# Local attention stage: softmax division moved from VectorE to GpSimd, norm floor by a second reduction, loop body of one group instead of two

## The chip, the cores and the metric

The kernel runs on one core of one Trainium2 chip. The metric is the device time of one execution, in microseconds (us); the number reported is the median of several runs. In what follows PE is TensorE (PEld its weight loads), DVE is VectorE, ACT is ScalarE, POOL is GpSimd and SP is SyncE, whose queue issues DMAs.

## The reference

The program keeps a residual x of 128 sequences of 64 tokens with 128 features and runs four pairs of layers over it: cross attention with a low-rank expert layer, with a mixture of experts, with a channel mixer, and last with two layers of local attention and a gated MLP. Only the local attention is touched by the change. It runs twice (DEPTH = 2), with 8 heads of 64 features:

```python
def l2norm(t):
    return t / jnp.clip(jnp.linalg.norm(t, axis=-1, keepdims=True), 1e-12)

def _layer(x, wqkv, qs, ksc, wo, lg, lb, w1, b1, w2, b2):
    h = shift_token(x)              # second half of the features from the token before
    q, k, v = jnp.split(h @ wqkv, 3, axis=-1)       # each b, 8 heads, n, 64
    q = l2norm(q) * qs
    k = l2norm(k) * ksc
    q, k = rotary_xpos(q, k)        # q * table_a + rotate_half(q) * table_b, the same for k
    o = local_attention(q, k, v)    # window 64 = the sequence: causal, softmax(8 * q k^T) @ v
    x = x + o @ wo
    ...                             # then the gated MLP, which the change leaves alone
```

## The kernel before

x stays in SBUF as 64 tiles of 128 rows (two sequences of 64 tokens) by 128 features. A group is 4 tiles (GT = 4), so there are 16 groups. `local_attention(l)` (from L1726) is written once per engine: each engine has a `body(g, par)` that loops over u = 0 to 3, and each step u works on several tiles at once, as a software pipeline over tiles. Tile n is the one whose attention ends in this step; n+1, n+2 and n+3 are in earlier phases. Engines meet only through semaphores (`wait_tile`), each engine does its work strictly in the order in which it is written, and that order is the only thing that sets the order of the work.

The way of one tile, with the names and lines as they stand in the profile:

- SP copies a group of x, with the shifted halves, into `hi` (the tensor `ci`), two buffers in turn (`move_shifted`, L1603, L1605). PE transposes the group into `bank_p` (L1788) and ACT copies it to `q_t` (L1902), two buffers in turn.
- `project_qk` (PE, L1796, L1797) writes q and k, 128x1024 in PSUM. `squares` (ACT, L1907) squares them. DVE multiplies them by the rotary tables: `rotate` (L2011) and two `cross` (L2018); POOL adds both (`unite`, L1970).
- `sum_squares` (DVE) sums the squares of each head (L2023) and then takes the maximum with 1e-24 and multiplies by 2^20 in one small instruction on 128x16 (L2026). `roots` (ACT, L1912, L1915) turns that into an inverse root by Ln and Exp, `refine_root` (POOL, L1976 to L1980) refines it in four small steps, and `scale_qk` (POOL, L1988) multiplies the rotated q and k with it. This last one gives the semaphore `unit`.
- `turn_qk` (PE, L1817) transposes q and k, `copy_qk` (ACT, L1926) copies them to SBUF, `scores` (PE, L1828 and L1836) multiplies them and adds the causal mask.
- The softmax: `maxima` (DVE, L2034), `shift` (DVE, L2039), `exponentials` (ACT, L1930), and `sums` (DVE), which is the sum (L2047), its reciprocal (L2049) and the division, a multiplication of 128x512 by the reciprocals (L2051).
- `turn_probs` (PE, L1847), `copy_pt` (ACT, L1935), `project_v` (PE, L1807) with `copy_v` (ACT, L1920), `weigh_values` (PE, L1861), `copy_ot` (ACT, L1940), `project_o` (PE, L1869), and `residual` (DVE, L2056).

Inside the stage, `run_pipeline` (L480 to L495) unrolls the first bodies and the last ones and runs the middle in a hardware loop whose body is two groups, 8 tiles, because the buffers of the groups alternate. The loop runs 7 times.

Of the kernel before, what the change touches and what calls it, by code (L numbers as in the profile page):

```python
# [85 lines left out]
def build_program(nc, w, x_in, ctx_t, mask_l2, mask_l3, out):  # L86

    with ExitStack() as ctx:
# [38 lines left out]
        big_flat = sb("big_flat", [P, 7 * INNER])  # L127
# [68 lines left out]
        top8 = sb("top8", [P, GT, 8])  # L196

# [1399 lines left out]
        def move_shifted(sp, last=False):  # L1597

            half = P // 2

            def load(g, par):
                rows = bass.ds(g * GT, GT)
                sp.dma_start(hi[par][:, :, 0:half], x[:, rows, 0:half]).then_inc(shift_loaded.sem, 16)  # L1603
                for b in range(2):
                    sp.dma_start(hi[par][b * S + 1:(b + 1) * S, :, half:P],  # L1605
                                 x[b * S:(b + 1) * S - 1, rows, half:P]).then_inc(shift_loaded.sem, 16)
# [4 lines left out]
            def body(g, par):  # L1611
# [7 lines left out]
                load(g + 2, par)  # L1619
# [17 lines left out]
        def prepare_layers():  # L1637

            with nc.Block() as block:
# [7 lines left out]
                def _(dve):  # L1647
                    for l in range(DEPTH):
# [77 lines left out]
        def local_attention(l):  # L1726
# [31 lines left out]
            nwork, nrm, nlog, nroot, nstep = (small[n][:, 0, :] for n in "abcde")  # L1758
# [15 lines left out]
            with nc.Block() as block:  # L1774
                @block.sync
                def _(sp):
                    move_shifted(sp)

                @block.tensor
                def _(pe):  # L1780
                    def tokens(t, par):
                        return q_t[(par + t // GT) % 2][:, t % GT * P:(t % GT + 1) * P]

                    def transpose_window(g, par):
                        pe.wait_ge(shift_loaded.sem, shift_loaded.at(g, 48))
                        wait_tile(pe, pt_copied, g, -GT)
                        for u in range(GT):
                            last = pe.transpose(bank_p[:, u * P:(u + 1) * P], hi[par][:, u, :], ident[:, :])  # L1788
                        last.then_inc(xt_in_psum.sem, 1)

                    def project_qk(g, t, par):
# [4 lines left out]
                        pe.matmul(bank_qk[:, 0, :], tokens(t, par), w_qkv[l][:, 0:INNER], start=True, stop=True)  # L1796
                        pe.matmul(bank_qk[:, 1, :], tokens(t, par), w_qkv[l][:, INNER:2 * INNER],  # L1797
                                  start=True, stop=True).then_inc(qk_in_psum.sem, 1)

                    def project_v(g, t, par):  # L1800
                        wait_tile(pe, v_copied, g, t - 1)
                        pe.sem_inc(pe_turn.sem, 1)
                        h = tokens(t, par)
# [46 lines left out]
                    def weigh_values(g, t):  # L1850
# [22 lines left out]
                    def body(g, par):  # L1873
                        for u in range(GT):
                            now, next_ = has_tile(g, u), has_tile(g, u + 1)
                            if has_tile(g, u + 3):
                                project_qk(g, u + 3, par)
                            if next_:
                                scores(g, u + 1)
                            if now:  # L1880
                                turn_probs(g, u)
                            if next_:
                                project_v(g, u + 1, par)
                            if now:
                                weigh_values(g, u)
                            if u == 0 and has(g + 1):
                                transpose_window(g + 1, 1 - par)
# [5 lines left out]
                    run_pipeline(pe, body, 1)  # L1893

                @block.scalar
                def _(act):
                    act.preload_act_table_set(LN_EXP)

                    def copy_window(g, par):
                        act.wait_ge(xt_in_psum.sem, xt_in_psum.at(g, 1))  # L1900
                        wait_tile(act, v_in_psum, g, -GT - 1)
                        act.activation(q_t[par][:, :], bank_p, ACT.Copy).then_inc(xt_ready.sem, 1)  # L1902
# [39 lines left out]
                    def body(g, par):  # L1942
# [398 lines left out]
```

## Time and profile before

| | us |
|---|---|
| median of 3 runs (lowest, highest) | 3454.64 (3454.24, 3457.28) |
| the profiled execution | 3454.24 |
| its span, first to last instruction | 3452.6 |
| PE busy in the span | 3039.5 (88%) |
| DVE busy | 2674.7 (77%) |
| ACT busy | 1624.8 (47%) |
| POOL busy | 895.3 (26%) |
| mean granted clock of TensorE | 0.951 of full speed |

The busy shares are over the whole program, of which the two local attentions are about a third: they stand at 2044 to 2585 us and at 2736 to 3298 us of the span. What holds a stage is read from that stretch alone, and in a pipeline over tiles from the time between equal instructions of neighbouring tiles. A row of the timeline gives an instruction's start and its duration; neighbouring DVE instructions overlap by some 0.1 us, so the cost of one in a full queue is the distance from its start to the start of the next.

### The profile page before, as it was taken

The numbers are of one execution on the slowest core, as the hardware profiler recorded it, in microseconds if no ns is written. First come the engines' busy times: TensorE is split into PE (matmuls) and PEld (weight loads), VectorE is DVE, ScalarE is ACT, GpSimd is POOL, SyncE is SP. The second block draws the span as 40 slices with busy tenths as digits, with TensorE's granted clock in tenths as the row PEclk, the third lists the DMA queues.
The fourth block names the chain that finished last, engine by engine and source line by source line (L and its number), as shares of the span: only waits on it lengthen the run. The fifth ranks groups of instructions, "written<-read, shape, count | busy, mean of one in ns | idle before, by whom it ended". The sixth has DMA issues, their size and how long they took to land. (4 is left out here: it accounts for less than half of the span.)

```text
span 3452.6 us, 95073 instructions
## 1 busy us (share of the span) xinstructions
PE 3039.5 (88%) x34096; PEld 2055.4 (60%) x34128; DVE 2674.7 (77%) x5823; ACT 1624.8 (47%) x2545; POOL 895.3 (26%) x940
## 2 busy tenths in 40 slices
PE   4999668998999979998799938898889888888889
PEld 2666555665666646666566626666655465656655
DVE  5887776886777757776588859999986599899965
ACT  2665214654333335553356625555553355555533
POOL 1000000000000000000100036666652266666634
PEclk9999668998999989999899969999999999999999
DMA  4111001110000011110011110000001100000022
GB/s 141 30 29 22 0 3 29 29 29 10 1 0 0 0 29 41 40 38 2 16 27 29 28 58 11 8 7 9 6 4 32 23 11 8 11 8 11 2 70 76
DMA packets 193348, 80.30 MB, mean 23 GB/s; under 512 B 179155, under 2 KB 182149, under 8 KB 192517
## 3 DMA queue, kind: packets, MB, share of 16 engines
q1 hardware_dynamic: 191876, 73.38, 9.1%
q0 software_dynamic: 1280, 4.20, 0.3%
q8 instruction: 142, 2.33, 0.3%
q14 instruction: 50, 0.40, 0.0%
HBM read 35.71 MB, written 8.39 MB: 13 GB/s over the span
## 5 line engine op out<-in xcount | busy, mean ns | idle before, releaser
L768 ACT ACTIVATE probs_t<-ps_pt 128x1024 f32<-128x1024 f32 x256 | 262.2, 1024 | 385.5 <-PE ps_pt L882 385.5
L630 DVE TENSOR_REDUCE row_max<-ps_s 128x16 f32<-128x1024 f32 x256 | 313.1, 1223 | 135.4 <-PE ps_s L871 132.4
L1970 POOL TENSOR_TENSOR kblk<-kblk 128x1024 f32<-128x1024 f32 x128 | 301.5, 2356 | 191.1 <-DVE kblk L2011 191.1
L635 DVE TENSOR_TENSOR probs<-ps_s,row_max 128x1024 f32<-128x1024 f32 x256 | 311.9, 1218 | 11.7
L614 POOL TENSOR_TENSOR x<-x,out_bias_L 128x512 f32 (+1 forms) x32 | 40.7, 1271 | 1028.4 <-DVE x_norm L424 519.8
L904 PE MATMUL ps_o<-v,probs_t 128*64 128x18 f32 x8192 | 285.1, 212 | 5.4 <-issue 5.2
L904 PEld LDWEIGHTS ps_o<-v,probs_t 128*64 128x64 f32 x8192 | 259.7, 138 | 40.3 <-issue 18.8
L882 PE MATMUL ps_pt<-ident,probs 128*128 128x128 f32 x2048 | 277.1, 278 | 3.1 <-ACT probs L763 3.1
L871 PE MATMUL ps_s<-kblk,q_t 64*64 64x512 f32 x2048 | 271.7, 603 | 7.0 <-issue 7.0
L763 ACT ACTIVATE probs<-probs 128x1024 f32<-128x1024 f32 x256 | 269.7, 1053 | 15.6 <-DVE probs L635 14.1
L1988 POOL TENSOR_TENSOR kblk<-kblk,small_d 128x1024 f32<-128x1024 f32 x128 | 243.6, 1903 | 50.6 <-POOL small_d L1980 50.6
L882 PEld LDWEIGHTS ps_pt<-ident,probs 128*128 128x128 f32 x2048 | 223.1, 141 | 36.7 <-issue 23.8
L1560 POOL TENSOR_TENSOR probs<-probs 128x512 f32<-128x512 f32 x16 | 16.8, 1048 | 866.6 <-ACT probs L1537 866.6
L2018 DVE TENSOR_TENSOR kblk<-ps_s,rot 128x512 f32<-128x512 f32 x256 | 173.5, 679 | 31.7 <-ACT probs L1907 31.6
L1325 ACT ACTIVATE probs<-ps_s 128x512 f32<-128x512 f32 x128 | 76.5, 597 | 226.3 <-PE ps_pt L1272 170.7
L2026 DVE TENSOR_SCALAR small_b<-small_a 128x16 f32<-128x16 f32 x128 | 169.7, 1326 | 15.0
L1817 PE MATMUL ps_s<-ident,kblk 128*128 128x128 f32 x1024 | 139.3, 280 | 38.2 <-POOL kblk L1988 37.1
L1926 ACT ACTIVATE big_flat<-ps_s 128x1024 f32<-128x1024 f32 x128 | 131.3, 1026 | 82.0 <-PE ps_s L1817 82.0
L1907 ACT ACTIVATE probs<-ps_s 128x1024 f32<-128x1024 f32 x128 | 131.0, 1024 | 79.4 <-PE ps_s L1797 75.1
L1869 PE MATMUL ps_pj<-w_lo,big_flat 128*128 128x128 f32 x1024 | 138.8, 279 | 32.1 <-ACT big_flat L1940 32.1
L1281 PEld LDWEIGHTS ps_o<-w,probs 128*128 128x128 f32 x1024 | 133.0, 191 | 49.5 <-issue 25.5
L891 PEld LDWEIGHTS ps_pt<-ident,o 128*128 128x128 f32 x256 | 35.4, 138 | 212.1 <-issue 123.3
(305 smaller groups left out, 6879.2 us busy)
## 6 DMA issues: line engine op xcount, KB each, us to landing
ci<-in_ctx_t SPq DMA_DIRECT2D x64, 256.0 KB, 3.0
kblk<-k_t SPq DMA_DIRECT2D x768, 16.0 KB
ci<-x SPq DMA_DIRECT2D x64, 128.0 KB
ci<-x SPq DMA_DIRECT2D x128, 63.0 KB
x<-in_x_in SPq DMA_DIRECT2D x4, 1024.0 KB, 8.1
mask<-in_mask_l SPq DMA_DIRECT2D x64, 64.0 KB, 2.5
kblk<-ci SPq DMA_DIRECT2D x256, 16.0 KB
out<-x SPq DMA_DIRECT2D x1, 4096.0 KB, 11.1
```

What stands on the lines that cost most here:

```text
L630: dve.tensor_reduce(row_max[u % 2][:, :], scores_of(u), AX, ALU.max).then_inc(max_ready.sem, 1)
L635: dve.tensor_tensor(probs[u % 2][:, :, :], scores_of(u), row_max[u % 2][:, :].unsqueeze(2).broadcast_to([P, HEADS, S]), ALU.subtract).then ...
L763: act.activation(p, p, ACT.Exp, scale=scale).then_inc(exp_ready.sem, 1)
L768: act.activation(probs_t[:, :, :], ps_pt[:, :, :].rearrange("p a (r t) -> p (a r) t", t=P), ACT.Copy).then_inc(pt_ready.sem, 1)
L871: last = pe.matmul(bank[b * S:(b + 1) * S, c, :], q_t[par][rows, tok], kblk[par][rows, :, tok], start=plain, stop=True, skip_group_check=n ...
L882: last = pe.transpose(ps_pt[:, r // 4, (r % 4) * P:(r % 4 + 1) * P], flat[:, r * P:(r + 1) * P], ident[:, :])
L904: last = pe.matmul(accumulated[half, 2 * r:2 * r + 2, :], probs_t[:, r, half], v2[par][:, 2 * u + b, r, :, :], start=True, stop=True)
L1817: last = pe.transpose(bank_ts[:, i, r * P:(r + 1) * P], rotated_qk[t % 2][:, i * INNER + r * P:i * INNER + (r + 1) * P], ident[:, :])
L1970: pool.tensor_tensor(a, a, b_, ALU.add).then_inc(rotated.sem, 1)
L1988: pool.tensor_tensor(a, a, nroot.unsqueeze(2).broadcast_to([P, 2 * LHEADS, LD]), ALU.mult)\
L2018: dve.tensor_tensor(b_[:, :, :, to:to + HALF], by_half(bank_qk)[:, :, :, of:of + HALF], table(1, to, HALF), ALU.mult).then_inc(products.se ...
L2026: dve.tensor_scalar(nrm, nwork, 1e-24, float(2 ** LOG_SCALE), ALU.max, ALU.mult)\
```

## The change

Six things change, all in `local_attention` or for it:

1. The division goes from DVE to POOL: `sums` ends with the reciprocal, and a new `scale_probs` (POOL) multiplies the 128x512 probabilities. The reciprocals have two places in turn.
2. The floor of the norms is no longer a `tensor_scalar` (maximum, then times 2^20) but a second `tensor_reduce` with maximum over pairs: the sums are written to column 0 of the new tensor `floored` (128x16x2), whose column 1 holds 1e-24. The factor 2^20 goes into ACT's Ln (as its scale) and into POOL's third refining step.
3. The order of DVE: maxima, shift, sums and reciprocal of tile n+1 in one stretch, then rotate, cross, cross and the norms of tile n+3; before, the two were interleaved.
4. The order of PE and ACT: `turn_probs` of tile n+1 ends a step (before, that of tile n stood behind the scores), scores come first, and V is projected and copied three tiles ahead, beside q and k, where it was one tile ahead. So `v_rows` needs four places instead of two; they are put over `kblk0`, and `big_flat` shrinks from 7 to 5 blocks.
5. POOL's `refine_root` and `scale_qk` become one `normalise_qk` for tile n+2, with two semaphore increments fewer.
6. `run_tiles` replaces `run_pipeline` here: a loop of one group (4 tiles) that runs 14 times, with one buffer `hi[0]` and one `q_t[0]` instead of two; SP's `move_window` loads a group once the one before it is transposed.

```diff
-            nwork, nrm, nlog, nroot, nstep = (small[n][:, 0, :] for n in "abcde")
+            nrm, nlog, nroot, nstep = (small[n][:, 0, :] for n in "bcde")
...
+        def run_tiles(eng, body):
+            for g in range(-1, 1):
+                body(g)
+            with eng.Fori(1, GROUPS - 1) as g:
+                body(g)
+            body(GROUPS - 1)
...
+        def move_window(sp):
+            def body(g):
+                if has(g + 1):
+                    if has(g):
+                        sp.wait_ge(xt_in_psum.sem, xt_in_psum.at(g, 1))
+                        sp.sem_inc(sp_turn.sem, 1)
+                    load_shifted(sp, g + 1, 0)
...
                 def _(dve):
+                    dve.memset(floored[:, :, 1], 1e-24).then_inc(tables.sem, 1)
...
-                                    at = t % 2 * INNER + b * 2 * P + r * LD
+                                    at = t % GT * INNER + b * 2 * P + r * LD
...
                     def roots(g, t):
                         wait_tile(act, norms, g, t)
-                        act.activation(nlog, nrm, ACT.Ln).then_inc(l_root.sem, 1)
+                        act.activation(nlog, nrm, ACT.Ln, scale=float(2 ** LOG_SCALE)).then_inc(l_root.sem, 1)
...
                     def copy_v(g, t):
                         wait_tile(act, v_in_psum, g, t)
-                        wait_tile(act, summed, g, t - 2)
-                        act.activation(v_rows[:, t % 2 * INNER:(t % 2 + 1) * INNER], bank_v, ACT.Copy)\
+                        wait_tile(act, summed, g, t - GT)
+                        act.activation(v_rows[:, t % GT * INNER:(t % GT + 1) * INNER], bank_v, ACT.Copy)\
...
-                    def body(g, par):
+                    def body(g):
                         for u in range(GT):
-                            now, soon = has_tile(g, u), has_tile(g, u + 2)
-                            if soon:
-                                roots(g, u + 2)
+                            now, next_ = has_tile(g, u), has_tile(g, u + 1)
+                            if next_:
+                                exponentials(g, u + 1)
                             if has_tile(g, u + 3):
                                 squares(g, u + 3)
                             if now:
-                                copy_pt(g, u)
+                                copy_ot(g, u)
+                            if has_tile(g, u + 3):
+                                copy_v(g, u + 3)
                             if u == 0 and has(g + 1):
-                                copy_window(g + 1, 1 - par)
-                            if has_tile(g, u + 1):
-                                exponentials(g, u + 1)
-                            if now:
-                                copy_ot(g, u)
-                            if soon:
+                                copy_window(g + 1)
+                            if has_tile(g, u + 2):
                                 copy_qk(g, u + 2)
-                            if has_tile(g, u + 1):
-                                copy_v(g, u + 1)
+                            if has_tile(g, u + 3):
+                                roots(g, u + 3)
+                            if next_:
+                                copy_pt(g, u + 1)
...
+                    def scale_probs(g, t):
+                        wait_tile(pool, rec_ready, g, t)
+                        pool.sem_inc(pool_turn.sem, 1)
+                        inverse = row_max[1][:, t % 2 * LHEADS:(t % 2 + 1) * LHEADS]
+                        p3 = by_head(pl)
+                        pool.tensor_tensor(p3, p3, inverse.unsqueeze(2).broadcast_to([P, LHEADS, S]), ALU.mult)\
+                            .then_inc(p_scaled.sem, 1)
...
-                        dve.tensor_reduce(nwork, square, AX, ALU.add).then_inc(norms.sem, 1)
+                        dve.tensor_reduce(floored[:, :, 0], square, AX, ALU.add).then_inc(norms.sem, 1)
                         wait_tile(dve, norms, g, t, 1)
                         wait_tile(dve, l_newton, g, t - 1)
-                        dve.tensor_scalar(nrm, nwork, 1e-24, float(2 ** LOG_SCALE), ALU.max, ALU.mult)\
-                           .then_inc(norms.sem, 1)
+                        dve.tensor_reduce(nrm, floored[:, :, :], AX, ALU.max).then_inc(norms.sem, 1)
```

How the instructions of one tile stand on three engines before and now, in the middle of the stage. POOL first: `kblk` holds the rotated q and k, `small_d` and `small_e` the root and its refining step, `big_flat` the probabilities. Before:

```order
L1988 TENSOR_TENSOR kblk<-kblk,small_d 128x1024 [waits l_newton,rotated]
L1970 TENSOR_TENSOR kblk<-kblk 128x1024 [waits products]
L1976 TENSOR_TENSOR small_e<-small_d 128x16 [waits l_root]
L1977 TENSOR_TENSOR small_e<-small_e,small_b 128x16 [waits l_newton]
L1979 TENSOR_SCALAR small_e<-small_e 128x16 [waits l_newton]
L1980 TENSOR_TENSOR small_d<-small_d,small_e 128x16 [waits l_newton]
```

and now, with the probabilities' scaling in front of the addition of tile n+2:

```order
L1993 TENSOR_TENSOR big_flat<-big_flat,row_max 128x512 [waits rec_ready]
L2000 TENSOR_TENSOR kblk<-kblk 128x1024 [waits products]
L2006 TENSOR_TENSOR small_e<-small_d 128x16 [waits l_root]
L2007 TENSOR_TENSOR small_e<-small_e,small_b 128x16 [waits l_newton]
L2009 TENSOR_SCALAR small_e<-small_e 128x16 [waits l_newton]
L2010 TENSOR_TENSOR small_d<-small_d,small_e 128x16 [waits l_newton]
L2013 TENSOR_TENSOR kblk<-kblk,small_d 128x1024 [waits rotated,l_newton]
```

One instruction of 128x512 is added, between two big ones that were neighbours. On DVE, one step before:

```order
L2034 TENSOR_REDUCE row_max<-ps_s 128x8 [waits scored]
L2018 TENSOR_TENSOR kblk<-ps_s,rot 128x16x32 [waits rotated,l_squared]
L2039 TENSOR_TENSOR big_flat<-ps_s,row_max 128x2x4x64 [waits turned,max_ready]
L2018 TENSOR_TENSOR kblk<-ps_s,rot 128x16x32 [waits rotated,l_squared]
L2011 TENSOR_TENSOR kblk<-ps_s,rot 128x1024 [waits qk_turned,l_squared]
L2023 TENSOR_REDUCE small_a<-probs 128x16 [waits l_squared]
L2026 TENSOR_SCALAR small_b<-small_a 128x16 [waits l_newton,norms]
L2047 TENSOR_REDUCE row_max<-big_flat 128x8 [waits exp_ready]
L2049 RECIPROCAL row_max<-row_max 128x8 [waits sums_ready]
L2051 TENSOR_TENSOR big_flat<-big_flat,row_max 128x512 [waits rec_ready]
L2056 TENSOR_TENSOR x<-x,ps_pj 128x128 [waits y_ready]
```

and now:

```order
L2057 TENSOR_REDUCE row_max<-ps_s 128x8 [waits scored]
L2060 TENSOR_TENSOR big_flat<-ps_s,row_max 128x2x4x64 [waits turned,max_ready]
L2068 TENSOR_REDUCE row_max<-big_flat 128x8 [waits p_scaled,exp_ready]
L2070 RECIPROCAL row_max<-row_max 128x8 [waits sums_ready]
L2036 TENSOR_TENSOR kblk<-ps_s,rot 128x1024 [waits qk_turned,l_squared]
L2043 TENSOR_TENSOR kblk<-ps_s,rot 128x16x32 [waits rotated,l_squared] x2
L2048 TENSOR_REDUCE floored<-probs 128x16 [waits l_squared]
L2051 TENSOR_REDUCE small_b<-floored 128x16 [waits l_newton,norms]
L2074 TENSOR_TENSOR x<-x,ps_pj 128x128 [waits y_ready]
```

The division (L2051 of before) is gone, the floor (L2026) is now a reduction (L2051 of the change), and the sum waits for `exp_ready` right behind the shift that ACT's exponential needs. On PE, one step before:

```order
L1796 MATMUL ps_s<-w_qkv,q_t 128x512
L1797 MATMUL ps_s<-w_qkv,q_t 128x512
L1828 MATMUL ps_s<-mask_causal,ident 64x256 x4
L1836 MATMUL ps_s<-big_flat 64x64 x16
L1847 MATMUL ps_pt<-ident,big_flat 128x128 x4
L1807 MATMUL ps_pt<-w_qkv,q_t 64x256 x4
L1861 MATMUL ps_o<-big_flat 64x64 x16
L1817 MATMUL ps_s<-ident,kblk 128x128 x8
L1869 MATMUL ps_pj<-w_lo,big_flat 128x128 x4
```

and now:

```order
L1851 MATMUL ps_s<-mask_causal,ident 64x256 x4
L1859 MATMUL ps_s<-big_flat 64x64 x16
L1819 MATMUL ps_s<-w_qkv,q_t 128x512
L1820 MATMUL ps_s<-w_qkv,q_t 128x512
L1830 MATMUL ps_pt<-w_qkv,q_t 64x256 x4
L1884 MATMUL ps_o<-big_flat,kblk 64x64 x16
L1840 MATMUL ps_s<-ident,kblk 128x128 x8
L1892 MATMUL ps_pj<-w_lo,big_flat 128x128 x4
L1870 MATMUL ps_pt<-ident,big_flat 128x128 x4
```

The same instructions in the same number; the transposition of the probabilities (L1847, now L1870) went from behind the scores to in front of the next tile's scores, and q, k and V of one tile now stand together.

## Rows read from the trace of the kernel before

**Rows 1.** The projections of q in the first and in the second local attention.

```profile
L1796 PE MATMUL ps_s<-w_qkv,q_t x128: 592/595/1222, 2049.9 to 2559.5; 128*128 128x512 f32 x128
...
L1796 PE MATMUL ps_s<-w_qkv,q_t x128: 592/595/1222, 2741.4 to 3271.9; 128*128 128x512 f32 x128
```

**Rows 2.** Timeline of DVE, one tile: start us, duration us, engine, line, operation.

```profile
2301.10 0.67 DVE L2047 TENSOR_REDUCE row_max<-big_flat 128x8 f32<-128x512 f32 x1
...
2302.04 0.69 DVE L2051 TENSOR_TENSOR big_flat<-big_flat,row_max 128x512 f32<-128x512 f32 x1
2302.65 0.28 DVE L2056 TENSOR_TENSOR x<-x,ps_pj 128x128 f32 x1
...
2305.34 1.21 DVE L2011 TENSOR_TENSOR kblk<-ps_s,rot 128x1024 f32<-128x1024 f32 x1
2306.47 1.21 DVE L2023 TENSOR_REDUCE small_a<-probs 128x16 f32<-128x1024 f32 x1
2307.82 1.30 DVE L2026 TENSOR_SCALAR small_b<-small_a 128x16 f32<-128x16 f32 x1
2309.03 0.67 DVE L2047 TENSOR_REDUCE row_max<-big_flat 128x8 f32<-128x512 f32 x1
...
2311.70 0.69 DVE L2034 TENSOR_REDUCE row_max<-ps_s 128x8 f32<-128x512 f32 x1 [0.84 <-PE ps_s L1836]
...
2312.91 0.68 DVE L2039 TENSOR_TENSOR big_flat<-ps_s,row_max 128x512 f32<-128x512 f32 x1
```

**Rows 3.** Timeline of POOL, one tile.

```profile
2306.73 2.35 POOL L1970 TENSOR_TENSOR kblk<-kblk 128x1024 f32<-128x1024 f32 x1 [0.96 <-DVE kblk L2011]
2309.86 0.22 POOL L1976 TENSOR_TENSOR small_e<-small_d 128x16 f32<-128x16 f32 x1 [0.77 <-ACT small_d L1915]
2310.16 0.59 POOL L1977 TENSOR_TENSOR small_e<-small_e,small_b 128x16 f32<-128x16 f32 x1
...
2311.80 1.91 POOL L1988 TENSOR_TENSOR kblk<-kblk,small_d 128x1024 f32<-128x1024 f32 x1 [0.35 <-POOL small_d L1980]
```

**Rows 4.** Timeline of PE, one tile without a group's transposition.

```profile
2309.05 1.02 PE L1796 MATMUL ps_s<-w_qkv,q_t 128*128 128x512 f32 x2
...
2310.86 0.30 PE L1828 MATMUL ps_s<-mask_causal,ident 64*64 64x256 bf16 x4
...
2311.56 0.65 PE L1847 MATMUL ps_pt<-ident,big_flat 128*128 128x128 f32 x4
2312.14 1.08 PE L1807 MATMUL ps_pt<-w_qkv,q_t 128*64 128x256 f32 x8
...
2314.24 1.09 PE L1817 MATMUL ps_s<-ident,kblk 128*128 128x128 f32 x8
2315.17 1.07 PE L1869 MATMUL ps_pj<-w_lo,big_flat 128*128 128x128 f32 x8
2316.07 0.59 PE L1796 MATMUL ps_s<-w_qkv,q_t 128*128 128x512 f32 x1
```

**Rows 5.** Timeline of ACT, two of its instructions there.

```profile
2310.97 1.02 ACT L1907 ACTIVATE probs<-ps_s 128x1024 f32<-128x1024 f32 x1 [1.28 <-PE ps_s L1797]
...
2313.62 0.63 ACT L1930 ACTIVATE big_flat<-big_flat 128x512 f32<-128x512 f32 x1 [0.78 <-DVE big_flat L2039]
```

**Rows 6.** DMA queue of instructions, 2040 to 2590 us and then 2740 to 3300 us.

```profile
q8 instruction: 13, 0.21, 0.2%
...
q8 instruction: 67, 1.10, 0.8%
```

**Rows 7.** Timeline of DVE and POOL side by side, normalising the residual before this stage.

```profile
2021.35 5.32 POOL L1692 TENSOR_TENSOR x<-x,probs 128x3072 f32<-128x3072 f32 x1 [11.60 <-DMA out<-x]
2021.38 10.64 DVE L1714 TENSOR_TENSOR x<-x,probs 128x5120 f32<-128x5120 f32 x1 [9.35 <-DMA out<-x]
```

**Rows 8.** Groups by line: a small DVE reduction, a full-stream POOL addition.

```profile
L1185 DVE TENSOR_REDUCE tiny_f<-small_b 128x4 f32<-128x16 f32 x16 | 2.7, 170 | 0.5
...
L2161 POOL TENSOR_TENSOR x<-x,b_dn 128x512 f32 x24 | 30.3, 1264 | 55.4 <-DVE x_norm L451 49.0 <-DMA ci<-x 6.4
```

More of the change, by code:

```diff
@@ L1595, in build_program, with load_shifted @@
         shift_loaded = signal("shift_loaded")
-        def move_shifted(sp, last=False):
[L1599 to L1606, printed above, removed]
+        def load_shifted(sp, g, par):
+            half = P // 2
+            rows = bass.ds(g * GT, GT)
+            sp.dma_start(hi[par][:, :, 0:half], x[:, rows, 0:half]).then_inc(shift_loaded.sem, 16)
+            for b in range(2):
+                sp.dma_start(hi[par][b * S + 1:(b + 1) * S, :, half:P],
+                             x[b * S:(b + 1) * S - 1, rows, half:P]).then_inc(shift_loaded.sem, 16)
+        def move_window(sp):
[5 more added lines that the diff above has]
+                    load_shifted(sp, g + 1, 0)
+            sp.wait_ge(first_rows.sem, 4)
+            run_tiles(sp, body)
+        def move_shifted(sp, last=False):
             def fetch(g, par):
@@ L1618, in body @@
                 sp.sem_inc(sp_turn.sem, 1)
-                load(g + 2, par)
+                load_shifted(sp, g + 2, par)
                 if last:
@@ L1776, in _, with tokens, transpose_window @@
                 def _(sp):
-                    move_shifted(sp)
+                    move_window(sp)
                 @block.tensor
                 def _(pe):
-                    def tokens(t, par):
-                        return q_t[(par + t // GT) % 2][:, t % GT * P:(t % GT + 1) * P]
-                    def transpose_window(g, par):
+                    def tokens(t):
+                        return q_t[0][:, t % GT * P:(t % GT + 1) * P]
+                    def transpose_window(g):
                         pe.wait_ge(shift_loaded.sem, shift_loaded.at(g, 48))
@@ L1787, in transpose_window, with project_qk @@
                         for u in range(GT):
-                            last = pe.transpose(bank_p[:, u * P:(u + 1) * P], hi[par][:, u, :], ident[:, :])
+                            last = pe.transpose(bank_p[:, u * P:(u + 1) * P], hi[0][:, u, :], ident[:, :])
                         last.then_inc(xt_in_psum.sem, 1)
-                    def project_qk(g, t, par):
+                    def project_qk(g, t):
                         if t % GT == 0:
@@ L1795, in project_qk, with project_v @@
                         wait_tile(pe, squared, g, t - 1)
[L1796 to L1797 removed]
+                        pe.matmul(bank_qk[:, 0, :], tokens(t), w_qkv[l][:, 0:INNER], start=True, stop=True)
+                        pe.matmul(bank_qk[:, 1, :], tokens(t), w_qkv[l][:, INNER:2 * INNER],
                                   start=True, stop=True).then_inc(qk_in_psum.sem, 1)
[L1800 removed]
+                    def project_v(g, t):
                         wait_tile(pe, v_copied, g, t - 1)
                         pe.sem_inc(pe_turn.sem, 1)
[L1803 removed]
+                        h = tokens(t)
                         w_v = w_qkv[l][:, 2 * INNER:3 * INNER].rearrange("p (r j d) -> p r j d", j=2, d=LD)
@@ L1897, in _, with copy_window @@
                     act.preload_act_table_set(LN_EXP)
-                    def copy_window(g, par):
+                    def copy_window(g):
                         act.wait_ge(xt_in_psum.sem, xt_in_psum.at(g, 1))
-                        wait_tile(act, v_in_psum, g, -GT - 1)
-                        act.activation(q_t[par][:, :], bank_p, ACT.Copy).then_inc(xt_ready.sem, 1)
+                        wait_tile(act, v_in_psum, g, -1)
+                        act.activation(q_t[0][:, :], bank_p, ACT.Copy).then_inc(xt_ready.sem, 1)
                     def squares(g, t):
@@ L1978, in refine_root @@
                         pool.sem_inc(pool_turn.sem, 1)
-                        step(pool.tensor_scalar(nstep, nstep, -0.5, 1.5, ALU.mult, ALU.add))
+                        step(pool.tensor_scalar(nstep, nstep, -0.5 * 2 ** LOG_SCALE, 1.5, ALU.mult, ALU.add))
                         step(pool.tensor_tensor(nroot, nroot, nstep, ALU.mult))
-                    def scale_qk(g, t):
                         wait_tile(pool, rotated, g, t)
-                        pool.sem_inc(pool_turn.sem, 1)
-                        wait_tile(pool, l_newton, g, t)
-                        pool.sem_inc(pool_turn.sem, 1)
                         a = by_head(rotated_qk[t % 2])
@@ L2223, in build_program @@
         qk_t = flat_big[:, 0:2 * INNER].rearrange("p (i t) -> p i t", i=2)
-        v_rows = flat_big[:, 2 * INNER:4 * INNER]
-        pl, pt, ot = (flat_big[:, i * INNER:(i + 1) * INNER] for i in (4, 5, 6))
+        pl, pt, ot = (flat_big[:, i * INNER:(i + 1) * INNER] for i in (2, 3, 4))
+        v_rows = kblk[0][:, :, :].rearrange("p h t -> p (h t)")[:, 0:GT * INNER]
         flat_parts = kblk[1][:, :, :].rearrange("p h t -> p (h t)")
```

67 lines of the change are left out of this document (29 added, 38 removed).

## Prediction

> **What bounds the kernel now.** The busy shares of the page do not say it: DVE 77%, PE 88% and POOL 26% are averages over eight stages, and the change touches two of them. I read first the line of one instruction that every tile has once, for the rate of the stage: the projection of q starts at 2049.9 for the first tile and at 2559.5 for the last of the first local attention, 509.6 us for 63 steps, 8.09 us a tile; in the second it is 530.5 us, 8.42 a tile [rows 1]. Together 1040.1 us for 126 steps, 8.25 a tile. Then the timeline engine by engine, for what each engine needs for a tile when nothing stops it, from start to start:
>
> - DVE: from one sum to the next, 2301.10 to 2309.03, 7.93 us without a gap [rows 2]. The next step has a wait of 0.84 us for the scores. So DVE is full, and its own 7.93 is nearly the whole 8.09.
> - PE: 2309.05 to 2316.07, 7.02 us for the same work [rows 4], plus a group's transposition (about 0.5) in one tile of four: 7.14. PE is second.
> - POOL: additions and multiplications of 2.35 and 1.91, a chain of four small steps between them, and waits for DVE and ACT [rows 3]. POOL is third.
>
> The second stage has the same engines and the same tiles, but is 20.9 us longer. What differs is the queue that fetches instructions: 13 packets in the first stage, 67 in the second [rows 6], on a loop of 8 tiles that turns 7 times. I read this as the loop's code being kept once and fetched again at each turn the other time, at 20.9 / 7 = 3.0 us a turn.
>
> **What the change does to each engine.** The division costs DVE 0.61 (2302.04 to 2302.65) [rows 2]; it goes. The floor costs it 1.21 (2307.82 to 2309.03), for 16 elements. That is a wait, not work: it ends at 2309.12 and POOL's addition ends at 2306.73 + 2.35 = 2309.08 [rows 2, 3]. Rows of another place show the same exclusion: DVE's subtraction of 5120 elements takes 10.64 beside a POOL operation of 5.32 that began 0.03 before it, where five times the 1.21 of 1024 elements would be 6.05 [rows 7, 2]. The new floor is a reduction of 32 elements to 16. No row shows one of this shape; a reduction of 16 elements takes 0.17 [rows 8] and I take 0.2. If it waits like the old one it costs 1.2; below 0.17 nothing speaks for it. Whether reductions wait is read off L1970: L2023, a reduction in SBUF, begins at 2306.47 and runs to 2307.68, POOL's addition begins inside it at 2306.73 and takes 2.35 for 1024 elements, where the one of L2161 takes 1.26 for 512 [rows 2, 3, 8]. So neither held the other up. DVE then needs 7.93 - 0.61 - 1.21 + 0.2 = 6.31 of work a tile. The new order adds waits, since the sum now stands right behind the shift: the exponential, 0.63 and 0.03 of handover on either side [rows 5], about 0.7; some 0.1 because the shift follows its maxima at once; and 0.1 for the squares, which ACT does after the exponential (1.02 [rows 5] against 0.94 for sum and reciprocal [rows 2]). DVE: 7.2.
>
> The Trainium skill says in "SBUF — State Buffer", section "SBUF: two separate sides", that the second port pair of VectorE is GpSimd's too and is locked for a whole instruction by a VectorE operation in a two-port mode or with two SBUF inputs; its "Vector Engine (DVE) Microarchitecture Reference", 5.1, gives those modes to copy, cast and tensor_scalar alone. By that the old floor waits and neither the reductions nor the reciprocal do, and the trace agrees for L2026 and L2023; by a lock that every SBUF-only operation took, the sum would be that of the slower rival below.
>
> POOL gains the division. It is the form of L1988, a broadcast multiplication, 1.91 for 1024 elements; L1970 and L2161, 2.35 for 1024 elements and 1.26 for 512, leave 0.17 that an instruction costs at any length [rows 3, 8]; (1.91 - 0.17) / 2 + 0.17 is 1.04. The bounds are 0.95 (half of 1.91) and 1.26, a POOL operation on 512 elements with two full streams [rows 8]. The small steps take 1.94 from 2309.86 to 2311.80; of this L1977 has 0.59 where its like L1976 has 0.22, held by DVE's division beside it, so 0.37 goes, and 0.2 of the 0.35 idle before L1988 goes with the two increments [rows 3]: 1.37. POOL: 2.35 + 1.91 + 1.04 + 1.37 + three handovers of 0.2 (the 0.18 below) = 7.27, the fullest engine. Where a page speaks against the change: "GPSIMD Engine Reference" of the Trainium skill, 4.1, sends elementwise work on a tile to VectorE, GpSimd being about twice slower. The row bears out less, 1.04 against 0.69 on DVE, because the second operand is a broadcast; at twice the DVE's 0.69, an estimate from that page, POOL would need 7.6.
>
> PE's work is the same, 7.14. ACT has two passes over 1024 elements at 1.02 and five over 512 at about 0.63 [rows 5], 5.2 with no more than two small ones besides, and is under the others.
>
> **The chain over engines.** Three engines at 7.1 to 7.3 do not run at 7.27 unless no chain between them is longer. The longest that I find goes round in two tiles. It starts when POOL has normalised q and k of tile k (0). PE starts 0.1 later and, in its new order, turns q and k (0.93), projects the output (0.90) and turns the probabilities (0.58) [rows 4]: 2.51, the scores of k begin. Maxima begin 0.84 after the scores [rows 2, 4]: 3.35; shift 0.72 later, 0.68 long [rows 2]: 4.75; exponential 0.03 + 0.63: 5.41; squares of k+2 on ACT 0.03 + 1.02 [rows 5]: 6.46, a little after sum and reciprocal (0.94, 6.38); rotate starts at 6.55 and takes 1.13 (2305.34 to 2306.47), the two crosses 0.60 and 0.68 [rows 2]: 8.96. POOL takes it up 0.18 later (2305.34 + 1.21 to 2306.73), adds 2.35, refines 0.1 + 1.37, multiplies 1.91 [rows 2, 3]: 14.87, the same point for k+2. So 7.43 a tile. In one tile of four ACT also copies the group's transposition (about 0.6) before the q and k that the scores need, of which some 0.45 is late: 0.11 a tile. Sum 7.54; I take 7.55.
>
> V three tiles ahead, its four places, the single `q_t` and `hi` cost nothing: the next group's load is asked for a whole group (30 us) before it is needed, and V's copy is ready three tiles early; without this cover each of the 32 groups would wait for its load, which no row here times. The memset of the floor is 0.1.
>
> **Code.** The loop is now 4 tiles and turns 14 times. Half the code should be kept in either stage, so the 20.9 us go; they are inside the sum, as both stages get 7.55.
>
> **Sum.** 126 x 7.55 = 951.3 against 1040.1: 88.8 less. Filling and draining hang on single chains and stay, 0.3 either way. From the profiled execution's 3454.24 (span 3452.6 and 1.6 around it; the median of the runs is 3454.64, 0.4 above): 3365.7, so 3366.
>
> **Rivals.**
> - *POOL alone sets the rate.* The two-tile chain has slack that I count twice, and all settle at 7.27. For it: my handovers are rounded up. 126 x 7.27 = 916.0: 3330.
> - *The reciprocal waits for POOL.* It is small, one-source and in SBUF like the old floor. At 6.1 of the chain POOL is in its last multiplication or just before; the rate would settle where the reciprocal slips in before it, 6.14 + 1.91 = 8.05. 126 x 8.05 = 1014.3: 3428. For it: no row shows a reciprocal in SBUF beside a long POOL operation. Against: L2023.
> - *The fetches stay.* The second loop is fetched anew at each of 14 turns at 3.0: 42 more: 3408. Against: 13 packets for a loop twice as long [rows 6].
> - *The floor does not get cheaper.* The reduction waits for POOL as the scalar form did, and the change doesn't do what it says: DVE at 7.2 + 1.1 = 8.3, 1045.8 in all: 3460, no change.
> - *Slower: all of DVE's SBUF-only operations exclude POOL.* POOL is busy 6.1 a tile, and the norms' reduction (1.21), the sum (0.67), the reciprocal and the floor (0.2 each) are 2.3. Before, POOL had the room to let them pass; now, with 1.1 of handovers, the tile takes 9.5: 126 x 9.5 = 1197, 157 more: 3611. It decides from 1.0 us of exclusion a tile (8.25 - 7.27). For it: L2026 and L1714 did wait. Against: L1970 beside L2023 did not grow.
>
> **How the numbers follow.** Forecast (7.4 to 7.75 a tile, 3347 to 3391) 0.64; POOL's rate 0.08; the reciprocal 0.11; fetches 0.08; floor 0.05; exclusion 0.04. This kernel's runs tell 0.2% (7 us) from no change. Faster is the forecast and the first three rivals, 0.91; same the floor, 0.05; slower 0.04. The range leaves out the first rival, the floor and the exclusion: 3338 to 3429. The unknown costs lie in it: a POOL division of 1.26 makes POOL 7.49, 0.95 makes it 7.18.
>
> **What would show it.** Starts of q's projection 7.5 us apart on average in both stages and some 30 us a group; DVE's floor at 0.2 and no longer ending with POOL's addition; POOL's division at 1.0 and L1977's like at 0.22; POOL over 90% occupied with waits for DVE's products before the addition; some ten or twenty instruction packets in either stage; no "issue" wait of 2 us before the projections. It is wrong if the reciprocal's rows exceed 0.3, if the floor's reach 1, or if PE's granted clock falls within the stages.

## The result and the profile after

| | before | changed |
|---|---|---|
| median, us (lowest, highest) | 3455.56 (3454.24, 3457.28), 4 runs | 3342.16 (3339.53, 3343.67), 4 runs |
| span of the profiled execution | 3452.6 | 3340.7 |
| mean granted clock of TensorE | 0.951 | 0.949 |

The ratio is 0.9671 (95% interval 0.9654 to 0.9687). The forecast was 3366 in a range of 3338 to 3429: the sign and the mechanism came, the gain was 24 us larger. The time is 4 us inside the range, and 5 us below the band of 3347 to 3391 that the forecast itself stood for. First the rate of the stage, as in [rows 1]:

```profile
L1819 PE MATMUL ps_s<-w_qkv,q_t x128: 592/697/1220, 2048.3 to 2515.0; 128*128 128x512 f32 x128
...
L1819 PE MATMUL ps_s<-w_qkv,q_t x128: 592/697/1222, 2695.8 to 3159.5; 128*128 128x512 f32 x128
```

466.7 and 463.7 us for 63 steps each, 930.4 together, where before there were 1040.1. That is 109.7 of the span's 111.9 us. The rest of the program kept its times. Per tile it is 7.41 and 7.36, against 8.09 and 8.42, and the second stage is no longer slower than the first. The queue that fetches instructions, 2040 to 2560 us and 2700 to 3200 us ([rows 6]), now looks the same in both stages:

```profile
q8 instruction: 10, 0.16, 0.1%
...
q8 instruction: 10, 0.16, 0.1%
```

The timeline of one tile, in the form of [rows 2 to 5], in the order of start times over all engines:

```profile
2320.17 1.05 POOL L1993 TENSOR_TENSOR big_flat<-big_flat,row_max 128x512 f32<-128x512 f32 x1
...
2320.34 1.09 PE L1840 MATMUL ps_s<-ident,kblk 128*128 128x128 f32 x8 [0.32 <-POOL kblk L2013]
...
2322.69 0.30 PE L1851 MATMUL ps_s<-mask_causal,ident 64*64 64x256 bf16 x4
...
2322.83 0.19 DVE L2051 TENSOR_REDUCE small_b<-floored 128x16 f32<-128x32 f32 x1
...
2323.53 0.69 DVE L2057 TENSOR_REDUCE row_max<-ps_s 128x8 f32<-128x512 f32 x1 [0.26 <-PE ps_s L1859]
...
2324.26 0.69 DVE L2060 TENSOR_TENSOR big_flat<-ps_s,row_max 128x512 f32<-128x512 f32 x1
...
2324.38 0.22 POOL L2007 TENSOR_TENSOR small_e<-small_e,small_b 128x16 f32<-128x16 f32 x1
...
2324.99 0.63 ACT L1952 ACTIVATE big_flat<-big_flat 128x512 f32<-128x512 f32 x1 [0.98 <-DVE big_flat L2060]
...
2325.46 1.90 POOL L2013 TENSOR_TENSOR kblk<-kblk,small_d 128x1024 f32<-128x1024 f32 x1 [0.16 <-POOL small_d L2010]
2325.52 1.00 ACT L1929 ACTIVATE probs<-ps_s 128x1024 f32<-128x1024 f32 x1
2325.65 0.69 DVE L2068 TENSOR_REDUCE row_max<-big_flat 128x8 f32<-128x512 f32 x1 [0.69 <-ACT big_flat L1952]
2326.32 1.15 PE L1884 MATMUL ps_o<-big_flat,kblk 64*64 64x64 f32 x32
2326.37 0.20 DVE L2070 RECIPROCAL row_max<-row_max 128x8 f32<-128x8 f32 x1
2326.56 1.23 DVE L2036 TENSOR_TENSOR kblk<-ps_s,rot 128x1024 f32<-128x1024 f32 x1
...
2327.70 1.28 DVE L2043 TENSOR_TENSOR kblk<-ps_s,rot 128x512 f32<-128x512 f32 x2
...
2329.16 2.37 POOL L2000 TENSOR_TENSOR kblk<-kblk 128x1024 f32<-128x1024 f32 x1 [0.79 <-DVE kblk L2043]
```

Three things are to be seen. The floor (L2051) takes 0.19 where it took 1.30, the division on POOL 1.05, and the step L2007 0.22 where L1977 took 0.59 [rows 2, 3]. The reciprocal (L2070) runs at 2326.37 for 0.20, in the middle of POOL's multiplication L2013 (2325.46 to 2327.36): it does not wait for it. And no engine sets the rate alone: DVE waits 0.69 for the exponential, POOL 0.79 for DVE's products, PE 0.32 for POOL. What sets the rate is the ring, the chain of waits through all four engines that comes back to its start.

### The profile page after: what moved, and what is told of

Its sections match the earlier page's. It is cut to its first block and busy times, and to the rows that moved or that the text cites. A ratio compares the mean times of both kernels' runs of the same rounds, so it can differ in the third digit from the quotient of the medians.

```text
span 3340.7 us, 95362 instructions
## 1 busy us (share of the span) xinstructions
PE 3035.8 (91%) x34128; PEld 2065.1 (62%) x34128; DVE 2487.0 (74%) x5696; ACT 1605.6 (48%) x2545; POOL 968.2 (29%) x1068
## 5 line engine op out<-in xcount | busy, mean ns | idle before, releaser
L2013 POOL TENSOR_TENSOR kblk<-kblk,small_d 128x1024 f32<-128x1024 f32 x128 | 243.5, 1902 | 19.0 <-POOL small_d L2010 17.7
L2036 DVE TENSOR_TENSOR kblk<-ps_s,rot 128x1024 f32<-128x1024 f32 x128 | 156.8, 1225 | 33.5 <-ACT probs L1929 33.5
L2043 DVE TENSOR_TENSOR kblk<-ps_s,rot 128x512 f32<-128x512 f32 x256 | 163.7, 681 | 0.0
L1884 PEld LDWEIGHTS ps_o<-big_flat,kblk 64*64 64x64 f32 x4096 | 129.6, 134 | 51.3 <-issue 51.3
L2068 DVE TENSOR_REDUCE row_max<-big_flat 128x8 f32<-128x512 f32 x128 | 87.8, 686 | 94.0 <-ACT big_flat L1952 94.0
L2048 DVE TENSOR_REDUCE floored<-probs 128x16 f32<-128x1024 f32 x128 | 154.7, 1209 | 0.0
```

Of the source, the lines that this page charges most:

```text
L2013: pool.tensor_tensor(a, a, nroot.unsqueeze(2).broadcast_to([P, 2 * LHEADS, LD]), ALU.mult)\
L2036: dve.tensor_tensor(a, by_half(bank_qk), table(0, 0, LD), ALU.mult).then_inc(products.sem, 1)
L2043: dve.tensor_tensor(b_[:, :, :, to:to + HALF], by_half(bank_qk)[:, :, :, of:of + HALF], table(1, to, HALF), ALU.mult).then_inc(products.se ...
L2048: dve.tensor_reduce(floored[:, :, 0], square, AX, ALU.add).then_inc(norms.sem, 1)
```

## The experiments

Eight kernels take the change apart, two more build on it. The measure beside the ratio is the sum of the two stages, first to last projection of q in the profiled execution, as in [rows 1]: 1040.1 before, 930.4 changed.

| kernel | median us | ratio (interval) | stages, us |
|---|---|---|---|
| floor alone | 3395.03 | 0.9825 (0.9809, 0.9842) | 483.3 + 503.1 |
| division alone | 3487.35 | 1.0100 (1.0083, 1.0117) | 529.5 + 543.7 |
| floor and division, old order | 3418.85 | 0.9894 (0.9878, 0.9911) | 493.6 + 514.3 |
| changed, old floor | 3446.36 | 0.9979 (0.9969, 0.9989) | 517.2 + 516.3 |
| changed, loop of two groups | 3382.89 | 0.9793 (0.9777, 0.9810) | 465.4 + 505.1 |
| changed, division on DVE | 3500.29 | 1.0137 (1.0120, 1.0154) | 543.0 + 542.2 |
| changed, less PE | 3340.55 | 0.9670 (0.9654, 0.9686) | 462.6 + 462.0 |
| changed, less POOL | 3324.46 | 0.9623 (0.9607, 0.9639) | 459.4 + 455.4 |
| addition in two halves | 3320.39 | 0.9614 (0.9601, 0.9627) | 456.6 + 455.4 |
| the same, less PE | 3323.33 | 0.9619 (0.9606, 0.9632) | 455.0 + 453.6 |

**Floor alone**, on the kernel before.

```diff
-    dve.tensor_scalar(nrm, nwork, 1e-24, float(2 ** LOG_SCALE), ALU.max, ALU.mult)
+    dve.tensor_reduce(nrm, floored[:, :, :], AX, ALU.max)
```

> The kernel before with the floor alone changed: the second reduction on 128x16x2 in place of the tensor_scalar, the factor 2^20 in Ln and in the refining step; old order, old loop, division on DVE. Theory (the floor was a wait for POOL's addition, and DVE set the rate): the floor's row falls from 1.3 to 0.19, DVE needs 6.9 a tile, PE's 7.14 takes over, some 7.4 a tile in the first attention; the second keeps its fetches, 3 us a turn. About 3370, 85 less than before. Rival (DVE full but the chains between engines hold the rate anyway): less than 30 gained, over 3425.

60 us went (54 of them in the two stages), the largest single part in the old order, but less than the 85 expected. Its waits, 2100 to 2500 us (engine and line, what it waited for, us in total, times, longest), show POOL waiting for DVE's products and DVE for PE's scores in turn; it runs at 7.67 a tile, between its engines' own 7.14 and the old 8.09:

```profile
POOL kblk L1972 <- DVE kblk L2013: 66.8, 53, 2.2
...
DVE row_max L2035 <- PE ps_s L1838: 37.4, 37, 1.8
```

**Division alone**, on the kernel before, between POOL's addition and its small steps.

```diff
-    dve.tensor_tensor(p3, p3, total..., ALU.mult)     # in sums
+    pool.tensor_tensor(p3, p3, inverse..., ALU.mult)  # scale_probs, after unite(g, u + 2)
```

> The kernel before with the division alone moved to POOL, placed between the addition of tile n+2 and its refining steps, reciprocals in two places; floor, order and loop as before. Theory: DVE needs 7.93 - 0.61 = 7.3 a tile, the floor still ends with POOL's addition (1.3), the refining of q and k comes 1.1 later on POOL but stays just in time: about 7.5 a tile, 3390. Rival: the 1.1 on POOL goes straight into the wait of PE for the normalised q and k, and most of the gain is given back: 3430 to 3460.

It is slower than before, by more than the rival had. DVE and POOL in the timeline:

```profile
2307.90 2.36 POOL L1978 TENSOR_TENSOR kblk<-kblk 128x1024 f32<-128x1024 f32 x1
...
2311.30 1.04 POOL L1971 TENSOR_TENSOR big_flat<-big_flat,row_max 128x512 f32<-128x512 f32 x1 [1.04 <-DVE row_max L2060]
...
2308.97 1.32 DVE L2037 TENSOR_SCALAR small_b<-small_a 128x16 f32<-128x16 f32 x1
2310.21 0.67 DVE L2058 TENSOR_REDUCE row_max<-big_flat 128x8 f32<-128x512 f32 x1
2310.91 0.20 DVE L2060 RECIPROCAL row_max<-row_max 128x8 f32<-128x8 f32 x1
```

The floor ends at 2310.29, with POOL's addition (2310.26); sum and reciprocal stand behind it, so POOL now waits 1.04 for the reciprocal, and then divides for 1.04, before it can refine and multiply. DVE's 0.61 was given back as 2.1 on POOL's path.

**Both, in the old order and loop.**

> Floor and division both changed as in the two kernels beside it, in the old order of all engines and the old loop of two groups. Theory: the two together take DVE to 6.3 a tile, PE sets the rate, and what the changed kernel has beyond is only the loop: 3342 + 21 = 3363. Rival: the new order is needed, since POOL's division in the old order delays q and k for PE: 3385 or more, no better than the floor alone.

The rival came: 24 us worse than the floor alone. DVE waits 79.5 us in 51 times for PE's scores there. So the division at this place pays nothing in the old order, with either floor. The changed kernel with a loop of two groups (below) differs from this one by the new order of four engines and the single buffers, and is 36 us faster. No run has the new order without the other changes, nor the new order and the single buffers apart.

**Changed, with the old floor** (and the factor 2^20 back in it).

```diff
-    dve.tensor_reduce(nrm, floored[:, :, :], AX, ALU.max)
+    dve.tensor_scalar(nrm, nwork, 1e-24, float(2 ** LOG_SCALE), ALU.max, ALU.mult)
```

> The changed kernel with the floor back as a tensor_scalar on 128x16 (maximum, times 2^20), all else as changed. Theory (the exclusion between DVE's one-source two-port operation and POOL): the floor starts while POOL adds and ends with it, 1.3 instead of 0.19; in the new order it stands in front of the maxima, so DVE's round grows to 8.2 a tile: about 3445. Rival (since PE sets the rate now, DVE has room): below 3365.

Met within 2 us. The form of one instruction on 16 elements is worth 104 us, by the waits behind it:

```profile
2302.60 1.32 DVE L2051 TENSOR_SCALAR small_b<-small_a 128x16 f32<-128x16 f32 x1
...
2301.53 2.36 POOL L2000 TENSOR_TENSOR kblk<-kblk 128x1024 f32<-128x1024 f32 x1 [0.77 <-DVE kblk L2043]
2304.59 0.21 POOL L2006 TENSOR_TENSOR small_e<-small_d 128x16 f32<-128x16 f32 x1 [0.71 <-ACT small_d L1937]
```

It ends 0.03 after the addition that it sat out (2303.89), and POOL, now on the ring, stands idle 0.71 for ACT's roots; with the reduction the root is there at 2323.52 (L1937), before the addition ends at 2324.12. That 0.71 and the later maxima (1.80 behind the scores' first matmul at 2302.23, where it was 0.84) make 8.20 a tile out of 7.38.

**Changed, with a loop of two groups** (SP's loop as changed).

```diff
-            with eng.Fori(1, GROUPS - 1) as g:
-                body(g)
+            with eng.Fori(1, GROUPS - 1, 2) as g:
+                body(g); body(g + 1)
```

> The changed kernel with the loop of two groups (8 tiles, 7 turns) on PE, ACT, POOL and DVE, SP's as changed; the order within a tile is the same. Theory (the code of the longer loop is fetched again at each turn in the second attention): 67 or so instruction packets there, stops of 2 us before the projections, about 7 x 3 = 21 us more: 3363, all of it in one of the two attentions. Rival (the fetches were no part of the gain, or jumps cost more than fetches): 3342 or less.

The first stage stays (465.4), the second grows by 41.4: 5.9 us a turn, twice the 3.0 expected. Its instruction queue has 13 and then 68 packets, and in the second stage PE stops twice in a turn, every 65 us (here without a releaser in the profile), where the changed kernel has no such stop:

```profile
2809.11 0.30 PE L1853 MATMUL ps_s<-mask_causal,ident 64*64 64x256 bf16 x4 [2.52 <-issue]
2811.92 0.69 PE L1861 MATMUL ps_s<-big_flat 64*64 64x64 f32 x12 [1.98 <-issue]
...
2874.47 0.43 PE L1853 MATMUL ps_s<-mask_causal,ident 64*64 64x256 bf16 x4 [2.33 <-issue]
2877.56 0.69 PE L1861 MATMUL ps_s<-big_flat 64*64 64x64 f32 x12 [2.02 <-issue]
```

The two stops are 4.4 to 5.3 us together. The rest is the clock: in the 5 us after the second stop TensorE's granted clock is 0.50 to 0.66 of full speed, in all six turns seen; 0.50 is the lower of its two levels, 1.2 of 2.4 GHz. The two projections take up to 2.07 and 1.91 where they take 1.12 and 1.02 at full speed. In the first row below stand the window, its length, the busy us of PE, PEld, DVE, ACT and POOL, the granted clock, the DMA share and GB/s:

```profile
2811.00:2816.00 5.00, 4.08 (x16) 1.67 (x15) 2.27 (x4) 0.63 (x1) 0.54 (x1) 0.50 0.02 3
...
2812.54 2.07 PE L1821 MATMUL ps_s<-w_qkv,q_t 128*128 128x512 f32 x2
...
2814.41 1.91 PE L1822 MATMUL ps_s<-w_qkv,q_t 128*128 128x512 f32 x2
```

That is 1.3 to 1.8 us more a turn. The kernel before has one such stop a turn, 1.8 to 2.4 us at L1796, and a clock of 0.66 behind four of the six and 1.00 behind two: so its turn costs less, 3.0. That the fetch is what stops PE is read from their coming and going together; the profile names no releaser. Why the first stage's loop of the same size is not fetched anew was not tried.

**Changed, with the division on DVE**, behind the reciprocal.

```diff
+    dve.tensor_tensor(p3, p3, total..., ALU.mult)     # in sums
-    scale_probs(g, u)                                 # on POOL
```

> The changed kernel with the division back on DVE, behind the reciprocal; POOL without it; floor, order and loop as changed. Theory: DVE's round grows by 0.6 to 7.8 a tile and passes PE's 7.3: 3342 + 126 x 0.45 = 3400. Rival (the floor and the order were all of the gain, the division's place none): within 10 of 3342.

100 us more than expected, for a reason not in the list:

```profile
2307.91 1.90 POOL L2013 TENSOR_TENSOR kblk<-kblk,small_d 128x1024 f32<-128x1024 f32 x1 [0.16 <-POOL small_d L2010]
...
2308.48 0.20 DVE L2068 RECIPROCAL row_max<-row_max 128x8 f32<-128x8 f32 x1
2308.71 1.65 DVE L2071 TENSOR_TENSOR big_flat<-big_flat,row_max 128x512 f32<-128x512 f32 x1
```

The division, with two operands in SBUF, takes 1.65 where it took 0.69 [rows 2], and finishes 0.55 after POOL's multiplication (2309.81 to 2310.36), while the reciprocal beside it is not held. In all 23 tiles from 2200 to 2400 us it falls on that multiplication, takes 1.18 to 1.65 and ends 0.54 to 0.56 behind it, so it sits out the overlap. POOL then waits 140.6 us in 46 times for DVE, 3.1 each (2100 to 2500 us). In this order the move to POOL is worth 158 us, 1.23 a tile in the stages; by the rows, the exclusion that it ends (0.49 to 0.96 of the division's time) counts about as much as the 0.61.

**Changed, less PE, and changed, less POOL.**

```diff
-    for r in range(LPAIRS):            # weigh_values, less PE
+    for r in range(LPAIRS // 2):
-    pool.tensor_tensor(a, a, b_, ALU.add)                                      # less POOL
+    pool.tensor_tensor(a[:, 0:INNER], a[:, 0:INNER], b_[:, 0:INNER], ALU.add)
```

The first leaves out half of the weighing of the values, the second half of the addition, so their output is incomplete.

> The changed kernel with half of the weighing of the values left out (8 of 16 matmuls of 64x64 a tile; the output is short of them): 0.58 us less PE a tile, all else the same. Theory A (PE sets the rate in the changed kernel, 7.17 for its work in the new order and 0.12 for the group's transposition; POOL's 7.27 comes next): 7.37 falls to about 7.25, 3326. Theory B (the prediction's chain over the engines sets it; the weighing is not in it): 3338 to 3343, nothing gained.

> The changed kernel with POOL's addition on half of its columns (k is left without its second product): 1.1 us less POOL a tile, all else the same. Theory A (PE sets the rate): 3335 to 3342. Theory B (POOL or the chain over the engines sets it; 1.1 less in a round of two tiles is 0.55 a tile, down to PE's 7.29): 3330 or less, with waits of PE for POOL gone.

Less PE gives nothing clear (1.6 us, inside the interval; 5.8 in the two stages), less POOL 17.7. So the ring through POOL sets the rate, and not PE, though PE is busy for 58.97 of 60 us in 2300 to 2360. But PE stands right behind. Taking 1.1 from POOL in a ring of two tiles could have given 0.55 a tile, 69 us, and gave 17.7. The busy times in 2740 to 3140 us of the changed kernel and of less POOL (PE, PEld, DVE, ACT, POOL):

```profile
2740.00:3140.00 400.00, 394.21 (x5510) 277.83 (x5507) 339.43 (x546) 254.27 (x452) 331.92 (x384) 1.00 0.04 9
...
2740.00:3140.00 400.00, 399.83 (x5607) 282.97 (x5604) 343.66 (x556) 257.06 (x459) 279.93 (x391) 1.00 0.04 9
```

With less POOL, PE is full and no longer waits for POOL, and four tiles take it 28.94 us (starts of L1819, 2305.47 to 2334.41): PE's own work in this order is 7.24 a tile, 0.14 under the changed kernel's 7.38.

**Addition in two halves**, a version meant to be better: the same work, the lower columns of each head added while DVE still makes the upper.

```diff
+    for half in range(2):
+        cols = slice(half * HALF, (half + 1) * HALF)
+        wait_tile(pool, products, g, t, 2 + half)
+        last = pool.tensor_tensor(a[..., cols], a[..., cols], b_[..., cols], ALU.add)
+    last.then_inc(rotated.sem, 1)
```

> The changed kernel with POOL's addition of rotated and crossed products cut in two: the lower 32 columns of each head once the first cross is there, the upper 32 once the second is. If the chain through POOL still sets the rate, it gets shorter by the second cross that the first half no longer waits for (0.68) less the second instruction's fixed cost (0.17), 0.5 in two tiles or 0.25 a tile: 7.38 becomes 7.29 at the least, where PE's own 7.17 + 0.12 stops it: 11 to 16 us less than the changed kernel's 3342, 3326 to 3331, ratio to before about 0.963, the figure of the kernel with half the addition. Rival: POOL is the full engine by its own work (additions, multiplications, division and small steps with their handovers), so that an instruction more costs it 0.2 to 0.35 a tile: 3365 to 3385.

> The same, and PE's weighing of V by the probabilities done for two of the four pairs of heads only (the rest of the output is stale). Alone this took nothing off the changed kernel. If with the shorter chain PE is the next limit, it must now pay: PE loses about 0.3 us a tile, and the rate falls from 7.29 to the shorter chain's 7.13: 20 us below the run without it, about 3307. Rival: the limit is still the chain or POOL itself, and it stays within 4 us of the run without it.

3320.39: 22 us under the changed kernel, the fastest here, with intervals of the ratio to before that do not touch. It runs at 7.24 a tile, under the 7.29 that I had taken for PE's floor, and less PE gives nothing again (7.21 a tile): PE is not the only limit. In its timeline POOL is nearly full:

```profile
2310.11 1.90 POOL L2017 TENSOR_TENSOR kblk<-kblk,small_d 128x1024 f32<-128x1024 f32 x1 [0.16 <-POOL small_d L2014]
2311.97 1.05 POOL L1993 TENSOR_TENSOR big_flat<-big_flat,row_max 128x512 f32<-128x512 f32 x1
2313.31 2.50 POOL L2003 TENSOR_TENSOR kblk<-kblk 128x512 f32<-128x512 f32 x2 [0.29 <-DVE kblk L2047]
...
2317.21 1.90 POOL L2017 TENSOR_TENSOR kblk<-kblk,small_d 128x1024 f32<-128x1024 f32 x1 [0.16 <-POOL small_d L2014]
```

From multiplication to multiplication 7.10, of it 0.29 idle for DVE. But PE is as full:

```profile
2740.00:3140.00 400.00, 399.72 (x5613) 282.84 (x5613) 343.80 (x558) 256.90 (x459) 348.49 (x446) 1.00 0.04 8
```

Two limits lie together here: the ring through POOL (7.21, the run with less PE) and PE's own 7.24 (the run with less POOL, which relieves POOL more than this one and is no faster). The next gain has to shorten both; no run does.

## Why the prediction was right, and where its 24 us are

- *DVE was the bound, the floor a wait for POOL.* That the floor was a wait and its removal pays is shown by the floor alone (60 us) and the old floor put back (104 us). That DVE's queue was the bound rests on [rows 2], where it has no gap; the runs do not part this from the other thing that an early floor does, namely ACT's roots come before POOL's addition ends (POOL waited 0.77 for them before [rows 3], 0.71 with the old floor put back). The floor's new price is 0.186, estimated at 0.2, in all 128 places. The reciprocal, my 0.11 rival, takes 0.203 in all of them. The price of POOL's division, 1.04, came as 1.047.
- *The rule on the shared port pair.* The Trainium skill, "SBUF — State Buffer", "SBUF: two separate sides", has the pair locked by two-port modes and by two SBUF inputs: the scalar floor at 1.32 beside the reduction at 0.186 and the reciprocal at 0.203 agree, and so does the division at 1.65 beside POOL's multiplication. I used the rule for the operations that stay on DVE and not for the division that leaves; the forecast did not need it, the expectation of its experiment did.
- *The chain over two tiles, 14.87 = 7.43 a tile.* Right in its kind (less PE nothing clear, less POOL 17.7 us) and 2% long. Where no loop turn lies between, it is 14.55, from 2318.31 to 2332.86 in the starts of L2013. By the rows above, with the end of the multiplication at 2320.21 as 0: scores 2.48, shift 4.05, exponential 4.78 to 5.41, as forecast; then squares 5.31 to 6.31 (forecast 6.46, they start 0.10 before the exponential's end), rotate 6.35 (6.55), addition 8.95 (9.14), the small steps and the multiplication with 0.13 less handover. One link differs: rotate follows the reciprocal (2326.37 + 0.20) and shows no wait, the squares are ready just before, where the forecast had the squares last. The mis-sized term is these handovers, 0.32 in two tiles: 0.16 x 126 = 20 of the 24 us; 2 more are the span outside the stages.
- *The engine behind the chain.* The prediction had POOL as the fullest engine at 7.27, and PE at 7.14. By the rows above POOL needs 6.60 (7.15 from multiplication to multiplication less 0.55 idle, the next 7.40 less 0.79): the three handovers of 0.2 in that sum are not there. PE needs 7.24. So the rival of POOL's rate had the wrong engine, though nearly the right figure, and the forecast did not rest on it.
- *0.11 a tile for the group's transposition.* The size nearly came, the cause did not, so that this term came near was luck. Four tiles take 29.53 (2303.33 to 2332.86), 0.43 more than 2 x 14.55, and the four before them 29.30 (2274.03 to 2303.33), 0.20 more: 0.08 a tile on average. At the loop's turn in the first of these groups the maxima come 1.13 after the scores' first matmul, where within a group they come 0.84 after:

```profile
2307.71 0.30 PE L1851 MATMUL ps_s<-mask_causal,ident 64*64 64x256 bf16 x4
...
2308.84 0.69 DVE L2057 TENSOR_REDUCE row_max<-ps_s 128x8 f32<-128x512 f32 x1 [0.21 <-issue]
...
2312.41 0.66 PE L1811 MATMUL ps_pt<-ident,ci 128*128 128x128 f32 x4
...
2312.91 1.04 PE L1840 MATMUL ps_s<-ident,kblk 128*128 128x128 f32 x8
```

  That is 0.29 for DVE's turn of the loop: with the loop of two groups the maxima are late (1.04 to 1.06) once in eight tiles, and 0.84 behind the scores at the group's start in the middle of the body. And PE starts to turn q and k 0.31 after POOL's multiplication ended (2312.60) instead of 0.13, because the transposition stands in front. In the other group it is 0.90 for the maxima and 0.53 for PE. ACT's copy, which I had named, is hardly late.
- *The fetches go.* Right: 10 packets in either stage. Before they cost 20.9 us by the difference of the stages; the changed order would have paid 41.4, so the short loop is worth twice what the step said: two stops a turn and the clock behind them, where the step had counted one price a turn from the kernel before. The total did not notice, since the forecast had both stages without them.
- *What the sum did not say.* The parts do not add. The floor is worth 60 in the old order and 104 in the new one; the division costs 33 alone and 24 on top of the floor, and is worth 158 in the new order; the short loop 41. (The recorded 3365.7 is a slip of 0.3: 3454.24 less 88.8 is 3365.4, and the median's 0.4 on top makes 3365.8.)

## What to carry to other kernels

Where all engines wait a little for one another, follow the ring through them to the same point one or two tiles later and add its links; shares of busy time do not name the bound (PE at 98% here was not it, but only 0.14 a tile from it), and a run that relieves one engine shows the next limit as well. Also, a few tenths of rounding up in the links are 2%. Moving work to another engine paid here only where the order was changed so that the receiver does it in a gap and its input is early: moving the same division lost 33 us or 24 us, or gained 158 us, by what stood around it. On DVE, put small SBUF work that must run beside long POOL operations in the form of reductions, and watch one-instruction waits that end with a POOL operation.

## What was not expected of the hardware

- A DVE multiplication with both inputs in SBUF (128x512) takes 1.65 beside a POOL operation that covers its first 1.10 us, and 0.69 where it starts outside one [rows 2]; a DVE reduction and a reciprocal in the same place take 0.69 and 0.20.
- A loop of 8 tiles is not refetched in the first stage and is in the second, in all kernels with that loop (13 packets against 67 to 69); with 4 tiles in neither (9 to 12). Beside the refetch PE stops once or twice a turn, for 1.8 to 2.8 us.
- After such stops TensorE's granted clock was 0.50 to 0.66 over 5 us, in ten of twelve turns of two kernels; its projections took up to 2.07 where they take 1.12.
- Turning the hardware loop costs DVE some 0.3 us where it is on the ring (the maxima up to 1.14 behind the scores, otherwise 0.84).
